# Language model tower on one core: second expert layer as split products, place map shared by two engines

## The reference

```python
logits = (x @ w_g).reshape(N, E)                      # N = 4096 tokens, E = 8 experts, K = 2
_, topk_idx = jax.lax.top_k(logits, K)
exp_rank = jnp.cumsum(exp_mask.reshape(K * N, E), axis=0) - 1
exp_mask = exp_mask * (exp_rank < cap).astype(jnp.int32)       # cap = 1280
...
xb = jnp.einsum('nec,nd->ecd', sec_mask, xf)          # the rows of each expert
h = jax.nn.gelu(jnp.einsum('ecd,edf->ecf', xb, fc_w) + fc_b, approximate=False)   # d = 192, f = 768
out = jnp.einsum('ecf,efd->ecd', h, pj_w) + pj_b
y = jnp.einsum('nec,ecd->nd', cb_weight, out)
```

## Time and profile before

| | |
|---|---|
| median of three runs | 1009.45 us (1009.11 to 1009.66) |
| profiled execution | 1016.04 us, span 1014.3 us |
| mean granted TensorE clock | 0.923 of full speed |
| TensorE busy | 897.5 us (88% of the span) |
| VectorE / ScalarE / GpSimd busy | 653.3 / 647.0 / 504.4 us |
| chain that ended last | PE 62%, DVE 13%, ACT 5% of the span |

### The profile page before, as it was taken

One profiled execution on the slowest core, in us unless ns is written; L12 is line 12 of the kernel. 1 busy time (PEld: TensorE's weight loads), 2 busy tenths in 40 slices (PEclk: granted clock), 3 DMA queues, 4 the chain that ended last, 5 costly groups with the idle time before them and its releaser, 6 DMA issues.

```text
span 1014.3 us, 21583 instructions
## 1 busy us (share of the span) xinstructions
PE 897.5 (88%) x7037; PEld 698.7 (69%) x7038; DVE 653.3 (64%) x3059; ACT 647.0 (64%) x1379; POOL 504.4 (50%) x549
## 2 busy tenths in 40 slices
PE   3387979999999979999999999367999999999996
PEld 2255556566666656677776776256999999999896
DVE  1676888998998877778877776673344343343341
ACT  2047778886989888988888889165345345344441
POOL 7677746765221201144234333415677677667654
PEclk8577998998999979999999999758999999999999
DMA  7234332322110200010011102427455456554443
GB/s 201 60 75 79 48 63 42 60 62 29 33 32 8 58 1 2 2 38 17 23 39 38 38 3 73 74 56 110 59 109 109 65 110 90 87 109 92 55 50 32
DMA packets 63300, 59.12 MB, mean 58 GB/s; under 512 B 17471, under 2 KB 54242, under 8 KB 63202
## 3 DMA queue, kind: packets, MB, share of 16 engines
q0 software_dynamic: 26624, 29.20, 20.0%
q1 hardware_dynamic: 36386, 28.44, 10.9%
q10 hardware_dynamic: 192, 0.26, 0.1%
HBM read 35.18 MB, written 16.39 MB: 51 GB/s over the span
## 4 chain that ended last, share of the span: by engine, by line
PE 62%; DVE 13%; ACT 5%; issue 3%; POOL 1%; DMA 0%; another core or an unknown queue 0%; POOLq 0%; DVEq 0%; ACTq 0%
PE ps_scores L798 14%; PE ps_ring L790 11%; PE ps_ring L1068 10%; PE ps_ring L798 6%; PE ps_ctx L927 5%; PE ps_scores L910 5%; PE ps_scores L1068 4%; PE ps_scores L913 4%; DVE probs L1456 2%; DVE probs L1470 1%; ACT probs L1170 1%; DVE k L1377 1%; PE ps_ring L873 1%; PE ps_ctx L790 1%; DVE probs L1450 1%
## 5 line engine op out<-in xcount | busy, mean ns | idle before, releaser
L1292 ACT ACTIVATE probs<-ps_scores,fc_bias 128x512 f32<-128x512 f32 (+1 forms) x144 | 88.7, 617 | 172.2 <-PE ps_scores L798 153.9
L661 POOL DMA_INDIRECT out<-z_t,slots_now x80 | 127.8, 1597 | 83.7 <-DVE z_t L1809 59.6
L1152 ACT ACTIVATE prob_t<-ps_ring 128x512 f32<-128x512 f32 x192 | 114.5, 597 | 36.0 <-PE ps_ring L790 35.4
L790 PE MATMUL ps_ring<-ident,probs 128*128 128x128 f32 x768 | 127.6, 292 | 9.0 <-DVE x_hi L1348 4.5
L1177 ACT ACTIVATE probs<-probs,neg_max 128x128 f32<-128x128 f32 x384 | 120.9, 398 | 2.6 <-DVE neg_max L1456 2.5
L1161 ACT ACTIVATE square<-ps_scores 128x512 f32<-128x512 f32 x192 | 104.9, 601 | 25.4 <-PE ps_scores L910 20.0
L1068 PE MATMUL ps_ring<-work,probs 128*128 128x192 f32 x672 | 114.5, 326 | 0.0
L790 PEld LDWEIGHTS ps_ring<-ident,probs 128*128 128x128 f32 x768 | 90.8, 147 | 34.1 <-issue 15.5
L1456 DVE CUSTOM_DVE_ANT_0 probs<-ps_scores,causal 128x128 f32<-128x128 f32 x384 | 88.5, 286 | 39.6 <-PE ps_scores L913 39.1
L1068 PEld LDWEIGHTS ps_ring<-work,probs 128*128 128x128 f32 x672 | 109.3, 190 | 0.1
L798 PE MATMUL ps_scores<-x_hi,fc_hi 128*128 128x512 f32 (+1 forms) x288 | 105.1, 371 | 3.8 <-DVE x_hi L1793 2.6
(11 more groups left out here) (232 smaller groups left out, 2074.0 us busy)
## 6 DMA issues: line engine op xcount, KB each, us to landing
work<-pj_w SPq DMA_DIRECT2D x8, 576.0 KB
k<-k_signed SPq DMA_DIRECT2D x136, 32.0 KB
token_in<-xin SPq DMA_DIRECT2D x8, 384.0 KB, 3.3
out<-resid SPq DMA_DIRECT2D x8, 384.0 KB, 4.2
vals<-fc_w SPq DMA_DIRECT2D x8, 384.0 KB
vals<-fc_w SPq DMA_DIRECT2D x16, 192.0 KB
k<-k_signed POOLq DMA_DIRECT2D x40, 32.0 KB, 2.0
out<-z_t,slots_now POOLq DMA_INDIRECT x80, 3.6
```

What stands on the lines that cost most here:

```text
L661: gp.indirect_dma_start(out[:, :], bass.IndirectOffsetOnAxis(slots_now[:, u, 1, t:t + 1], 0), slot_y[:, o, :], None, compute_op=ALU.add).t ...
L790: return pe.transpose(dst, src, ident[0:n, 0:n])
L1152: sc.activation(prob_t[:, s % 2, :, :], src.rearrange("p (h q) -> p h q", h=4), ACT.Exp if p is mag else ACT.Copy).then_inc(ring_free[i], 1)
L1292: sc.activation(hidden[:, c % 2, f_, 0:128 * nt], ps_scores[:, i, 0:128 * nt], ACT.Gelu, bias=fc_bias[:, e, f_:f_ + 1]).then_inc(gelu_done ...
```

## The change

Three parts.

**The second layer as split products.** ScalarE writes `hid_hi`, the hidden block rounded to fp32r, after each gelu (one group behind it), and VectorE writes the remainder `hid_lo`. The second weights are split too, once an expert: `pj_split` holds the high part in columns 0 to 191 and the low part in 192 to 383. TensorE multiplies `hid_hi` by all 384 columns and `hid_lo` by the first 192, six of each. The result then lies in two halves of a bank, and VectorE adds them with two additions before the bank is free.

**The place map.** `high_hot` is made by VectorE in one step (is_equal, then times the token number), four instructions of 80 columns a round. `low_hot` of even rounds is VectorE's as before; that of odd rounds is ScalarE's: |number - low| (four instructions), then relu(1 - that) (one). The ring has six places instead of three, some in the weight buffers of expert 1.

**One semaphore** `y_scaled` counts the results instead of five. SP waits for the split of the second weights (`pj_low`) instead of TensorE's start on the next expert before it loads new ones.

```diff
+        hid_hi = sb("hid_hi", [128, FF_CHUNKS, 512], F32R)
+        hid_lo = sb("hid_lo", [128, FF_CHUNKS, 512], F32R)
+        pj_split = sb("pj_split", [128, 2, FF_CHUNKS, 2 * HID], F32R)
...
-        PAIRS_AT_ONCE, HOT_RING = 4, 3
+        PAIRS_AT_ONCE, HOT_RING = 4, 6
...
@@ sync
-                sp.wait_ge(pj_used[e % 2], e // 2 + 1)
+                if e > 1:
+                    sp.wait_ge(pj_low, e - 1)
                 load_second_layer(e)
@@ gpsimd
-                pool.wait_ge(y_scaled[o], e * (CAP_TILES // OUT_RING) + t // OUT_RING + 1)
+                pool.wait_ge(y_scaled, e * CAP_TILES + t + 1)
@@ tensor, second_layer
                 if c == 0:
-                    pe.wait_ge(pj_loaded[u], 16 * r + 16)
+                    pe.wait_ge(pj_low, e + 1)
+                order = ([(hid_hi, hid_high, f_) for f_ in range(FF_CHUNKS - 1)]
+                         + [(hid_lo, hid_low, f_) for f_ in range(FF_CHUNKS)] + [(hid_hi, hid_high, FF_CHUNKS - 1)])
                 for t in range(t0, t0 + nt):
                     i, n = y_place(e, t)
                     pe.wait_ge(y_free[i], n + 1)
                     tok = slice(128 * (t - t0), 128 * (t - t0) + 128)
-                    for f_ in range(FF_CHUNKS):
+                    for k, (part, made, f_) in enumerate(order):
                         if t == t0:
-                            pe.wait_ge(gelu_done[f_ % FC_RING], e * 6 + 2 * c + f_ // FC_RING + 2)
-                        last = pe.matmul(ps_y[i][:, 0:HID], hidden[:, c % 2, f_, tok], pj_w_sb[:, u, f_, :],
-                                         start=(f_ == 0), stop=(f_ == FF_CHUNKS - 1))
+                            pe.wait_ge(made, e * 18 + 6 * c + f_ + 1)
+                        n = 2 * HID if part is hid_hi else HID
+                        last = pe.matmul(ps_y[i][:, 0:n], part[:, f_, tok], pj_split[:, u, f_, 0:n],
+                                         start=(k == 0), stop=(k == 2 * FF_CHUNKS - 1))
@@ scalar
-            for q in range(TOPK * SEQS // PAIRS_AT_ONCE):
-                act.wait_ge(ones_made, q + 1)
+            act.wait_ge(digits_made, 1)
+            for n, q in enumerate(range(1, TOPK * SEQS // PAIRS_AT_ONCE, 2)):
                 for j in range(PAIRS_AT_ONCE):
                     c = PAIRS_AT_ONCE * q + j
-                    last = sc.activation(high_hot[:, q % HOT_RING, j, :], high_one[:, q % HOT_RING, j, :], ACT.Copy,
-                                         scale=token_no[:, c:c + 1])
-                last.then_inc(hots_made, 1)
+                    last = sc.activation(away[:, n % 2, j, :], number, ACT.Abs, bias=at_f[:, 0, c:c + 1], scale=-1.0)
+                last.then_inc(away_made, 1)
+                act.wait_ge(away_made, n + 1)
...
+                sc.activation(low_hot[q % HOT_RING], away[:, n % 2, :, :], ACT.Relu, bias=one_f[:, 0:1], scale=-1.0
+                              ).then_inc(act_hots_made, 1)
...
+                    if f_ > 0:
+                        hidden_high(e, c, f_ - 1)
+                hidden_high(e, c, FF_CHUNKS - 1)
+
+            def hidden_high(e, c, f_):
+                tok = slice(0, 128 * CHUNKS[c][1])
+                act.wait_ge(gelu_done[f_ % FC_RING], e * 6 + 2 * c + f_ // FC_RING + 2)
+                apart(act)
+                sc.activation(hid_hi[:, f_, tok], hidden[:, c % 2, f_, tok], ACT.Copy).then_inc(hid_high, 1)
+
+            def second_weights_high(n, u):
+                act.wait_ge(pj_loaded[u], 16 * n + 16)
+                sc.activation(pj_split[:, u, :, 0:HID], pj_w_sb[:, u, :, :], ACT.Copy).then_inc(pj_high, 1)
...
@@ vector, route_tokens: the high tables
-                    ve.tensor_tensor(high_one[:, q % HOT_RING, :, :],
-                                     number[:, 0:HIGH].unsqueeze(1).to_broadcast([128, PAIRS_AT_ONCE, HIGH]),
-                                     high[:, some].unsqueeze(2).to_broadcast([128, PAIRS_AT_ONCE, HIGH]),
-                                     ALU.is_equal).then_inc(ones_made, 1)
+                    for j in range(PAIRS_AT_ONCE):
+                        c = PAIRS_AT_ONCE * q + j
+                        last = ve.tensor_scalar(high_hot[q % HOT_RING][:, j, :], number[:, 0:HIGH], high[:, c:c + 1],
+                                                token_no[:, c:c + 1], ALU.is_equal, ALU.mult)
+                    last.then_inc(hots_made, 1)
@@ vector, experts
-                        ve.tensor_tensor(slot_y[:, o, :], ps_y[i][:, 0:HID], pj_bias[:, e, :], ALU.add
+                        ve.tensor_tensor(slot_y[:, o, :], ps_y[i][:, HID:2 * HID], pj_bias[:, e, :], ALU.add
+                                         ).then_inc(y_begun, 1)
+                        dve.wait_ge(y_begun, CAP_TILES * e + t + 1)
+                        ve.tensor_tensor(slot_y[:, o, :], slot_y[:, o, :], ps_y[i][:, 0:HID], ALU.add
                                          ).then_inc(y_free[i], 1)
...
+                def hidden_low(e, c):
+                    tok = slice(0, 128 * CHUNKS[c][1])
+                    for f_ in range(FF_CHUNKS):
+                        dve.wait_ge(hid_high, e * 18 + 6 * c + f_ + 1)
+                        apart(dve)
+                        ve.tensor_tensor(hid_lo[:, f_, tok], hidden[:, c % 2, f_, tok], f(hid_hi[:, f_, tok]),
+                                         ALU.subtract).then_inc(hid_low, 1)
...
                 def expert(e, u, more):
+                    hidden_low(e, 0)
                     split_x(e, u, 1)
                     add_bias(e, u, 0)
                     if more:
                         split_weights(e + 1, 1 - u)
+                        second_weights_low(e + 1, 1 - u)
+                    hidden_low(e, 1)
                     split_x(e, u, 2)
                     add_bias(e, u, 1)
+                    hidden_low(e, 2)
                     if more:
                         split_x(e + 1, 1 - u, 0)
                     add_bias(e, u, 2)
```

More of the change, by code:

```diff
@@ L192, in tower_kernel @@
         resid = sb("resid", [128, SEQS, HID])
-        xin = sb("xin", [128, SEQS, WITH_GATE])
+        with ExitStack() as attention_only:
+            early = lambda name, shape, dt=F32: attention_only.enter_context(nc.sbuf_tensor(name, shape, dt))
+            q_of = [early(f"q{u}", [128, BLOCKS, GROUP, 128]) for u in range(2)]
+            k_of = [early(f"k{u}", [128, BLOCKS, 2, GROUP, 128]) for u in range(2)]
+            xin = early("xin", [128, SEQS, WITH_GATE])
+            w_hi = early("w_hi", [128, 2, 2, 384], F32R)
+            square = early("square", [128, 2, 4, 2, 128])
+        low_hot_at = sb("low_hot", [128, BLOCKS * GROUP * 128], F32R)
+        high_hot_at = sb("high_hot", [128, BLOCKS * GROUP * 128], F32R)
+        fc_hi = sb("fc_hi", [128, 2, 2, FF], F32R)
+        fc_lo = sb("fc_lo", [128, 2, 2, FF], F32R)
+        hid_hi = sb("hid_hi", [128, FF_CHUNKS, 512], F32R)
+        hid_lo = sb("hid_lo", [128, FF_CHUNKS, 512], F32R)
+        pj_split = sb("pj_split", [128, 2, FF_CHUNKS, 2 * HID], F32R)
         logits = sb("logits", [128, 2, EXPERTS])
@@ L282, in tower_kernel, with hot_places @@
         LOW, HIGH = 128, SLOTS // 128
-        PAIRS_AT_ONCE, HOT_RING = 4, 3
[L284 to L287, removed]
+        PAIRS_AT_ONCE, HOT_RING = 4, 6
+        def hot_places(tiles, n):
+            return [tile[:, PAIRS_AT_ONCE * n * i:PAIRS_AT_ONCE * n * (i + 1)].rearrange("p (c n) -> p c n", n=n)
+                    for tile in tiles for i in range(HOT_RING // 2)]
+        low_hot = hot_places((low_hot_at[:, :], fc_hi[:, 1, :, :].rearrange("p c n -> p (c n)")), LOW)
+        high_hot = hot_places((high_hot_at[:, :], fc_lo[:, 1, :, :].rearrange("p c n -> p (c n)")), HIGH)
         slots_now = sb("slots_now", [128, 2, 2, CAP_TILES], I32)
-        high_one = xn[:, :, :].rearrange("p s d -> p (s d)")[:, 0:HOT_RING * PAIRS_AT_ONCE * HIGH].rearrange(
-            "p (r c n) -> p r c n", r=HOT_RING, c=PAIRS_AT_ONCE)
+        away = xn[:, :, :].rearrange("p s d -> p (s d)").rearrange("p (r c n) -> p r c n", r=2, c=PAIRS_AT_ONCE)
         of_slot = scratch[:, 2, 0:240].rearrange("p (a n) -> p a n", a=3)
@@ L327, in tower_kernel @@
         bias_added = sem("bias_added")
-        y_scaled = [sem(f"y_scaled{i}") for i in range(5)]
+        y_scaled = sem("y_scaled")
         one_exp = sb("one_exp", [128, 1])
@@ L412, in tower_kernel @@
         pj_loaded = [sem(f"pj_loaded{u}") for u in range(2)]
-        pj_used = [sem(f"pj_used{u}") for u in range(2)]
+        pj_high = sem("pj_high")
+        pj_low = sem("pj_low")
+        hid_high = sem("hid_high")
+        hid_low = sem("hid_low")
+        y_begun = sem("y_begun")
         x_loaded = [sem(f"x_loaded{c}") for c in range(3)]
@@ L798, in split_product @@
                     last = pe.matmul(dst, lhs, rhs, start=(k == 0), stop=(k == 4))
-                    if begun is not None and k == 0:
-                        last.then_inc(begun, 1)
                 return last
@@ L1004, in _ @@
                 pe.wait_ge(hots_made, q + 1)
```

(6 more changed lines are left out.)

53 lines of the change are left out of this document (29 added, 24 removed).

## The result

The changed kernel takes 1031.24 us (median of four, 1026.01 to 1034.61) against 1009.56 (1009.11 to 1011.33): ratio 1.0193, interval 1.0162 to 1.0224. It is slower by 22 us; 1027 was predicted, 1014 to 1042. The profiled execution spans 1032.9 us, 18.6 more than that of before (1014.3).

The account below looks back on a forecast made before the run. TensorE bounds the eight experts, 39.2 us each; 2.4 saved against 4.4 waited gives +2.0 an expert, +16, plus 0.8 (ends) and 0.4 (place map): +17 to 18, so 1027 us on the median 1009.45, range 1014 to 1042.

Parts of the forecast that it names:

- Second-layer tile: TensorE, experts: 1.71 us a tile against 1.95, with 0.11 per 192-column product from an attention row; 2.4 saved an expert.
- Cost of copies and subtractions: New hidden and weight splits: ScalarE +9.4 us to 28, VectorE +14 to 30 of 39 an expert; neither becomes the bound.
- Waits of an expert: TensorE waits on the longer chain gelu, copy, subtraction, product: 4.25 us an expert, 4.4 with handovers.
- For x_hi 1.4: After chunk 0: VectorE ends the split of the next x at 859.4, TensorE wants it at 858.0; wait 1.4 us.
- Chunk 1 0.85 + 0.5: Chunk 1's second layer: TensorE waits 0.85 us for hidden copies and subtractions and 0.5 for a free bank.
- Chunk 2 1.3: Chunk 2's second layer: TensorE waits 0.7 us for copy 4 and 0.5 for subtraction 5, 0.1 between; 1.3 in all.
- Chunk 0 0.2: Chunk 0's second layer, two tiles: TensorE held about 0.2 us by the last hidden pieces.
- Place map, +0.4: Place map stage: VectorE becomes its bound, 19.7 us of tables, ending at 679.8 against 679.45; +0.4 us.
- Ends of the stage, +0.8: End of the expert stage: one more addition (0.36 us) and tiles coming faster than GpSimd's stores; +0.8 us in all.
- Semaphore, loads of weights: 0: One semaphore for a result's rows, same count and order; second weights' load released earlier by VectorE: 0 us.
- One sign of being wrong: Granted clock leaving 1.00 among the experts; rival of a falling clock, chance 0.15: four to eight experts, 1034 to 1041 us.
- GpSimd as the bound: Rival, chance 0.07: VectorE's two-input subtractions hold GpSimd's transfers in the experts; about 1050 us if each loses 0.6.

Follow-up runs that it names:

- pair_tiles: Changed kernel, but TensorE takes each chunk's first two tiles together, each hidden piece going to both before the next is waited for: 1026.77 us, ratio 1.0157.
- weights_early: Changed kernel, but VectorE makes a chunk's row weights ahead of that chunk's hidden subtractions, not between them and the split of x: 1024.58 us, ratio 1.0126.
- x_halves: Changed kernel, but in chunk 1 the first two first-layer pieces go in halves of 256 columns, each once its tile pair is split: 1025.02 us, ratio 1.0133.
- map_alone: Kernel before with only the new place map and the one semaphore, second layer as before: 1013.77 us, ratio 1.0023.
- low_by_copy: Changed kernel, but hid_lo is a one-input copy of the gelu's output, leaving out the subtraction: 1030.61 us, one run.

## Why the prediction was right

- *Second-layer tile, 1.71 us.* Measured 1.72. The row of 192 columns was the right one to take.
- *Cost of copies and subtractions.* Predicted for 512, 256 and 1152 columns on ScalarE 0.64, 0.43, 1.2, measured 0.621, 0.421, 1.190; on VectorE 0.69, 0.42, 1.35, measured 0.691, 0.424, 1.352.
- *Waits of an expert.* For x_hi 1.4 (1.42). Chunk 1 0.85 + 0.5 (1.36). Chunk 2 1.3 (1.30). Chunk 0 0.2 (0.61): the term that was too small here. Its excess is VectorE's late start on subtraction 4, 0.36 over the usual, and part of the 0.1 us by which a product after a wait gives way late. In the second expert and the last two chunk 0 and x_hi together cost 1.41 to 1.52, against 1.6 predicted. Sum 4.25, measured 4.69 in this stretch; period 41.3, measured 41.46 here and 41.30 on the mean without the clock's part.
- *What is luck in that.* The sums of chunks 1 and 2 agree to 0.02, their parts do not. I had TensorE wait for a copy twice an expert, 0.4 in chunk 1 and 0.7 in chunk 2. It did so once an expert, in chunk 2, for 0.40 (893.96 - 893.38 less 0.175); the subtractions, and the 0.1 us after each wait, took the rest. The list from 690 us on has it eight times, once an expert:

```profile
PE ps_ring L1079 <- ACT hid_hi L1318: 2.3, 8, 0.7
```

- *What showed the mechanism.* pair_tiles took out 0.5 to 0.9 us of chunk 2's 1.3, weights_early chunk 1's wait for a bank (its second layer 7.75 us for 8.25) and x_halves the wait for x_hi, and each moved the time in its direction.
- *Place map, +0.4.* 659.03 to 679.45 before; after, VectorE's first table starts at 658.20 and TensorE's last round ends at 679.07: 20.42 and 20.87 us. The 80-column table took 327 ns where I had 0.32. map_alone: +0.23% (0.06 to 0.40%), of which this is a fifth.

The last two rounds of the map in the changed kernel; TensorE waits for VectorE's table:

```profile
677.07 1.07 PE L1019 MATMUL ps_scores<-high_hot,low_hot 128*128 128x80 f32 x4 [0.45 <-DVE high_hot L1786]
678.00 1.07 PE L1019 MATMUL ps_scores<-fc_lo,fc_hi 128*128 128x80 f32 x4
```

- *Ends of the stage, +0.8.* From TensorE's last product to the end of the execution 8.10 us before and 8.97 after.
- *Semaphore, loads of weights: 0.* No wait on them in the lists; not run alone.
- *Time.* Predicted +17 to 18 on the profiled execution; it was 18.6: 14.8 for seven periods of 41.30 in place of 39.19, 1.7 for the clock, 2.5 for what lies before the first and after the last of them, and -0.4 until the stage begins. The 14.8 and the 2.5, less 0.9 for the end, are 16.4 for eight experts, against 16. The medians differ by 22, 1.93% where 1.7% was predicted. The attention's scatter between executions is of the size of these 4 us; no run divides them.
- *Signs and rivals.* One sign of being wrong did come: the clock left 1.00 among the experts, once in the profiled execution and not four to eight times. It cost 1.7 us that the forecast did not hold. The window shows TensorE 95% busy and not 89%; by the starts it is 36.77 of 41.46, which is 89%. GpSimd as the bound: no. What I did not have is how close the other side was: the same diff with six edits of order is faster than before by 1%.

## What to carry to other kernels

A cheaper product on a full engine pays only if what feeds it keeps its lead. Walk one period of the loop and write beside each product when it is wanted and when its input is there; here that gave 41.3, and the mean was 41.3, though the parts were shared out otherwise. When waits stand in series, taking one out pays in part, because the next stands close behind: look after each step at what the *feeding* engines wait for, not only at the busiest one. And a step that is moved forward takes its own wait along, in front of all that is queued behind it.

## What the runs showed of the hardware

- In the changed kernel 9 of 80 indirect stores on GpSimd issued for over 1.8 us (before 1), all beside VectorE's subtractions with two inputs in SBUF: five of 2.3 to 2.5 us beside the splits of weights, four of 2.0 to 2.1 beside the hidden subtractions. Two of them:

```profile
872.40 2.32 POOL L673 DMA_INDIRECT out<-z_t,slots_now  x1 [1.30 <-DVE z_t L1849]
875.02 2.11 POOL L673 DMA_INDIRECT out<-z_t,slots_now  x1 [0.30 <-issue]
```

  The Trainium skill, page "SBUF — State Buffer", section "Who interferes with whom", says that a VectorE instruction with two SBUF inputs contends with a GpSimd instruction that reads SBUF. These rows agree in part: 47 other stores took at most 1.60 us, though 23.7 us of such subtractions lay beside them. In low_by_copy, with one-input copies for the hidden subtractions, the three longest stores (2.53 to 2.54 us) are still there beside the splits of weights, and no other took over 1.82.
- After a wait of 1.4 us the first 512-column product started its successor 0.33 us later (869.34, next at 869.67); with no wait ahead it was 0.23 (885.44, 885.67). A pause is not needed for it: in the kernel before, behind the float32 products and with no wait, it was 0.37 (858.20, 858.57).
